# GpSimd makes the first norm's rows, half of the convolution and half of the softplus; two table loads fewer; scales read as pairs

## The reference, cut to what matters

```
x = x + tanh(g_xattn[0]) * attention(layernorm(x), ctx)      # softmax over 256 keys of each batch
x = x + tanh(g_ffn[0])   * ternary_ffn(layernorm(x))         # weights rounded to -s, 0, s; s = mean |w| of 64
x = x + tanh(g_xattn[1]) * ssm(ctx, z=layernorm(x))          # conv of 4 taps, silu, softplus, 16 states, scan
x = x + tanh(g_ffn[1])   * moe(layernorm(x))                 # 64 experts, top 8, capacity 128

# inside ssm
u     = silu(conv1d(in_proj_w @ ctx, conv_w, 4 taps, causal) + conv_b)
delta = softplus(dt_proj_w @ (x_proj_w @ u)[:8] + dt_proj_b)
# inside ternary_ffn, for each group of 64 weights
scale = clip(mean(abs(w)), 1e-8);  q = clip(round(w / scale), -1, 1);  w_hat = q * scale
```

## Time and profile before

| | us |
|---|---|
| median of 3 runs | 412.1 (411.82 to 413.02) |
| profiled execution, span | 411.6 |
| ACT busy | 263.1 |
| DVE busy | 305.4 |
| POOL busy | 260.1 |
| PE busy | 338.7 |

### The profile page before, as it was taken

How to read it: one execution, slowest core, us unless ns; L and a number is a source line. 1 busy time by engine, 2 the same in 40 slices (tenths; PEclk the granted TensorE clock), 3 DMA queues, 4 the chain that set the end, 5 groups by cost and what they waited for, 6 DMA issues and landing times.

```text
span 411.6 us, 7573 instructions
## 1 busy us (share of the span) xinstructions
PE 338.7 (82%) x2217; PEld 267.8 (65%) x2217; DVE 305.4 (74%) x694; ACT 263.1 (64%) x530; POOL 260.1 (63%) x213
## 2 busy tenths in 40 slices
PE   4945974698789799989885189999999999999980
PEld 2431663256566567666685178899998899899870
DVE  2999999979999999999888946554544535454365
ACT  0899999999888898888264344445445544554410
POOL 4200022679996897788423588778788787878730
PEclk9995895599999989989999579999999999999997
DMA  8930530577344877441198339899898989865557
GB/s 235 372 121 0 152 114 3 183 224 244 118 153 130 273 259 260 154 146 59 42 263 204 104 105 209 219 212 241 202 238 219 221 216 217 224 139 94 96 107 241
DMA packets 59132, 72.17 MB, mean 175 GB/s; under 512 B 6802, under 2 KB 43458, under 8 KB 59106
## 3 DMA queue, kind: packets, MB, share of 16 engines
q1 hardware_dynamic: 49104, 56.04, 44.2%
q0 software_dynamic: 8832, 15.74, 19.1%
q10 hardware_dynamic: 1170, 0.08, 0.3%
HBM read 61.75 MB, written 10.09 MB: 175 GB/s over the span
## 4 chain that ended last, share of the span: by engine, by line
PE 50%; ACT 15%; DVE 14%; DMA 12%; issue 5%; POOL 2%; SPq 1%; DVEq 0%; POOLq 0%; ACTq 0%
PE bank L1328 13%; PE bank L1366 10%; PE bank L1321 6%; PE bank L1162 5%; DMA ssm<-bc_rows 4%; PE bank L1308 3%; DVE bank L1565 3%; DMA B_last<-bc_rows 3%; ACT ssm L862 2%; ACT L862 2%; DVE ssm L1570 2%; ACT L900 2%; DMA du<-sums 2%; PE bank L1104 2%; PE bank L1314 1%
## 5 line engine op out<-in xcount | busy, mean ns | idle before, releaser
L602 POOL TENSOR_TENSOR ssm<-ssm,arena 128x1024 f32<-128x1024 f32 x31 | 73.2, 2360 | 18.8 <-DVE ssm L1570 9.3
L1570 DVE TENSOR_TENSOR_SCAN ssm<-ssm,bank 128x512 f32<-128x512 f32 x64 | 78.1, 1220 | 4.6 <-issue 2.3
L675 POOL DMA_INDIRECT ssm<-routed,idx x64 | 65.0, 1016 | 21.8 <-issue 14.6
L1793 DVE SCALAR_TENSOR_TENSOR ssm<-ssm,bank 128x96 f32<-128x96 f32 x64 | 20.1, 314 | 75.3 <-ACT ssm L974 75.0
L686 POOL DMA_INDIRECT sums<-ssm,idx x40 | 65.3, 1631 | 13.6 <-issue 10.4
L1328 PE MATMUL bank<-ssm,wguT 128*128 128x256 bf16 x576 | 72.4, 272 | 0.3 <-DVE ssm L1785 0.3
L1328 PEld LDWEIGHTS bank<-ssm,wguT 128*128 128x128 bf16 x576 | 56.0, 97 | 12.3 <-DVE ssm L1785 0.7
L974 ACT ACTIVATE ssm<-bank 128x96 f32<-128x96 f32 x64 | 16.1, 251 | 74.3 <-PE bank L1366 74.3
L1162 PE MATMUL bank<-xs,wguT 128*128 128x512 bf16 x192 | 49.4, 412 | 7.8 <-POOL xs L589 4.2
L1366 PE MATMUL bank<-arena,ssm 128*128 (+1 forms) x256 | 53.3, 331 | 1.8 <-ACT ssm L957 1.1
L862 ACT ACTIVATE ssm<-delta,A_sb 128x510 f32<-128x510 f32 x64 | 43.9, 714 | 6.1 <-DVE ssm L1570 5.9
(11 more groups left out here) (226 smaller groups left out, 667.9 us busy)
## 6 DMA issues: line engine op xcount, KB each, us to landing
ssm<-bc_rows SPq DMA_DIRECT2D x22, 512.0 KB, 3.8
arena<-bc_rows SPq DMA_DIRECT2D x16, 512.0 KB, 5.1
arena<-in_L_ffn_gate_proj SPq DMA_DIRECT2D x32, 192.0 KB
arena<-in_L_ffn_up_proj SPq DMA_DIRECT2D x32, 192.0 KB
arena<-in_L_ffn_down_proj SPq DMA_DIRECT2D x32, 192.0 KB
B_last<-bc_rows SPq DMA_DIRECT2D x10, 512.0 KB, 3.8
sums<-zero_f SPq DMA_DIRECT2D x1, 2304.0 KB, 14.0
arena<-in_L_ffn_w_gate_up SPq DMA_DIRECT2D x1, 2048.0 KB, 11.6
```

Source lines behind the costliest of these rows:

```text
L602: pool.tensor_tensor(prod[:, a:b, :], hs[:, a:b, :], C_all[:, 2 * (q % 8):2 * (q % 8) + 2, :], ALU.mult).then_inc(s.prod_ok, 1)
L675: pool.indirect_dma_start(out=xe[:, k, :], out_offset=None, in_=routed, in_offset=bass.IndirectOffsetOnAxis(ap=idx2[:, k, 0:1], axis=0)).t ...
L1570: dve.tensor_tensor_scan(hs[:, k % 4, :], dA[:, k % 3, :], x[:, :], 0.0, ALU.mult, ALU.add).then_inc(s.scan_ok, 1)
```

## The change

- Norm 1's rows are made by POOL (`normalise(c)`, four TENSOR_SCALAR of 256 columns for each chunk), between and behind the two `ln_rstd(1, ...)`. DVE's eight operations of L1415 are gone.
- `convolve_second` on POOL makes half 1 of the convolution: one TENSOR_SCALAR, then three pairs of TENSOR_SCALAR (a tap into `delta[:, 1]`, free then) and TENSOR_TENSOR (the sum), 1024 columns each, with waits between them. ACT's silu of half 1 waits for its semaphore.
- ACT's `spread` is gone. `q_scale` holds each scale twice, and `rest_and_mask` subtracts |w| from the scales read through an access pattern of (group step 2) x (32 times the same) x (2 adjacent bf16).
- `softplus_second` on POOL, between `ln_rstd(2, (0,))` and `ln_rstd(2, (1,))`: two TENSOR_SCALAR and two TENSOR_TENSOR of 1024 columns; behind `ln_rstd(2, (1,))` POOL also makes `delta[:, 1]` with a third TENSOR_TENSOR. DVE keeps half 0, moves `quantised(1)` ahead of `nmr` 1, and makes `delta[:, 0]` behind it.
- ACT loads a table by name at the very start (`exp_and_others`) and ahead of the softplus exponentials (`natural_log_exp_and_others`, which has Exp and Ln), so that the loads at L809 and at the first decay aren't needed. The decays of phase 0 wait for `delta[:, 0]` alone.

```diff
+            def normalise(c):
+                pool.wait_ge(s.ln_r, c + 1)
+                for j in range(4 * c, 4 * c + 4):
+                    pool.tensor_scalar(xn[j], x_res[:, j, :], mv[:, j, 0:1], rstd[:, j:j + 1], ALU.subtract, ALU.mult).then_inc(s.xn_sb, 1)
+            def convolve_second():
+                pool.wait_ge(s.ld_cols, 16 * 4)
+                pool.wait_ge(s.wT_sb, 3)
+                pool.wait_ge(s.xin_sb, 4)
+                ub, tap = (v[:, 1, :].rearrange("p (b l) -> p b l", l=L) for v in (u, delta))
+                for k in range(DC):
+                    src = xin[:, 1, :, k:k + L]
+                    if k == 0:
+                        pool.tensor_scalar(ub, src, conv_sb[:, 1, 0:1], cols[:, 1:2], ALU.mult, ALU.add).then_inc(s.conv_second, 1)
+                    else:
+                        if k > 1:
+                            pool.wait_ge(s.conv_second, 2 * k - 1)
+                        pool.tensor_scalar(tap, src, conv_sb[:, 1, k:k + 1], None, ALU.mult).then_inc(s.conv_second, 1)
+                        pool.wait_ge(s.conv_second, 2 * k)
+                        pool.tensor_tensor(ub, tap, ub, ALU.add).then_inc(s.conv_second, 1)
-            ln_rstd(1)
-            ln_rstd(2)
+            ln_rstd(1, (0,))
+            normalise(0)
+            ln_rstd(1, (1,))
+            normalise(1)
+            convolve_second()
+            def softplus_second():
+                pool.wait_ge(s.sp_exp, 2)
+                pool.tensor_single_scalar(Bbc[:, 1, :], delta[:, 1, :], 1.0, op=ALU.add).then_inc(s.sp_second, 1)
+                pool.wait_ge(s.sp_second, 1)
+                pool.tensor_single_scalar(Bbc[:, 1, :], Bbc[:, 1, :], -1.0, op=ALU.add).then_inc(s.sp_second, 1)
+                pool.wait_ge(s.sp_second, 2)
+                pool.tensor_tensor(Bbc[:, 1, :], Bbc[:, 1, :], delta[:, 1, :], ALU.subtract).then_inc(s.sp_second, 1)
+                pool.wait_ge(s.sp_second, 3)
+                pool.wait_ge(s.sp_relu, 4)
+                pool.tensor_tensor(Bbc[:, 1, :], du[:, 1, :], Bbc[:, 1, :], ALU.subtract).then_inc(s.sp_second, 1)
+            ln_rstd(2, (0,))
+            softplus_second()
+            ln_rstd(2, (1,))
+            pool.wait_ge(s.sp_second, 4)
+            pool.wait_ge(s.sp_ln, 2)
+            pool.tensor_tensor(delta[:, 1, :], Cbc[:, 1, :], Bbc[:, 1, :], ALU.add).then_inc(s.delta_second, 1)
...
+            act.preload_act_table_set("exp_and_others")
             act.wait_ge(s.c_pad, 1)
...
-            spread(0)
             for j in range(NT):
                 act.wait_ge(s.en_max, 2 * (j // 2) + 2)
...
             for h in halves:
-                act.wait_ge(s.conv, 4 * h + 4)
+                act.wait_ge((s.conv, s.conv_second)[h], (DC, 2 * DC - 1)[h])
                 act.activation(u[:, h, :], u[:, h, :], ACT.Silu).then_inc(s.u_sb, 1)
-            spread(1)
...
+            act.preload_act_table_set("natural_log_exp_and_others")
             for h in halves:
                 act.wait_ge(s.sp_abs, 2 * h + 2)
...
-            act.wait_ge(s.delta_sb, 2)
+            act.wait_ge(s.delta_sb, 1)
...
-                dve.wait_ge(s.q_mat, part2 + 1)
-                dve.tensor_tensor(q_v[:, t], q_v[:, t], q_abs[:, t], ALU.subtract).then_inc(s.q_step, 1)
+                dve.wait_ge(s.q_scales, 2 * part2 + 2)
+                dve.tensor_tensor(v_pairs[:, g], over_group(part2), q_pairs[:, g], ALU.subtract).then_inc(s.q_step, 1)
...
             statistics(2, x1, s.x1_sb, (0,))
-            softplus_rest(0, lambda: mean_over_deviation(2, 0))
+            softplus_first()
+            mean_over_deviation(2, 0)
             statistics(2, x1, s.x1_sb, (1,))
-            softplus_rest(1, lambda: mean_over_deviation(2, 1))
-            for h in halves:
-                dve.wait_ge(s.sp_c, 3 * h + 3)
-                dve.wait_ge(s.sp_ln, h + 1)
-                dve.tensor_tensor(delta[:, h, :], Cbc[:, h, :], Bbc[:, h, :], ALU.add).then_inc(s.delta_sb, 1)
             quantised(1)
+            mean_over_deviation(2, 1)
+            dve.wait_ge(s.sp_c, 3)
+            dve.wait_ge(s.sp_ln, 1)
+            dve.tensor_tensor(delta[:, 0, :], Cbc[:, 0, :], Bbc[:, 0, :], ALU.add).then_inc(s.delta_sb, 1)
```

More of the change, by code:

```diff
@@ L117, in __init__ @@
         self.sp_c = sem("sp_c")
+        self.sp_second = sem("sp_second")
+        self.delta_second = sem("delta_second")
         self.sp_ln = sem("sp_ln")
@@ L284, in build @@
         qg = q_abs.rearrange("p (g n) -> p g n", n=GROUP)
-        vg = q_v.rearrange("p (g n) -> p g n", n=GROUP)
+        in_pairs = "p (g n two) -> p g n two"
+        q_pairs, v_pairs = (v.rearrange(in_pairs, n=GROUP // 2, two=2) for v in (q_abs, q_v))
         q_groups = (slice(0, 16 * D // GROUP), slice(16 * D // GROUP, NG))
         q_sum = sb("q_sum", [P, NG])
-        q_scale = sb("q_scale", [P, NG], BF16)
+        q_scale = sb("q_scale", [P, NG, 2], BF16)
         stats = sb("stats", [P, NT, 6])
@@ L391, in over_group @@
             g = q_groups[part2]
-            return part(q_scale[:, g.start:g.start + 1], (1, g.stop - g.start), (0, GROUP))
+            return part(q_scale[:, g.start, 0:1], (2, g.stop - g.start), (0, GROUP // 2), (1, 2))
         s = Semaphores(sem)
@@ L859, in decay @@
                 th, h, n, t = of_step(k)
+                if k == DS:
+                    act.wait_ge(s.delta_second, 1)
                 if k >= 3:
@@ L1410, in _ @@
         def _(dve):
-            def normalise(n, c):
-                for j in range(4 * c, 4 * c + 4):
-                    dve.wait_ge(s.ln_r, 2 * n - 1 + j // 4)
-                    dve.tensor_scalar(xn[j], x_res[:, j, :], mv[:, j, 0:1], rstd[:, j:j + 1], ALU.subtract, ALU.mult).then_inc(s.xn_sb, 1)
             def statistics(n, update=None, updated=None, chunks=(0, 1)):
@@ L1444, in _, with convolve_first @@
             statistics(1)
-            normalise(1, 0)
-            normalise(1, 1)
             dve.wait_ge(s.ld_cols, 16 * 4)
             dve.wait_ge(s.wT_sb, 3)
-            def convolve(h):
-                dve.wait_ge(s.xin_sb, 2 * h + 2)
-                ub = u[:, h, :].rearrange("p (b l) -> p b l", l=L)
+            def convolve_first():
+                dve.wait_ge(s.xin_sb, 2)
+                ub = u[:, 0, :].rearrange("p (b l) -> p b l", l=L)
                 for k in range(DC):
-                    src = xin[:, h, :, k:k + L]
+                    src = xin[:, 0, :, k:k + L]
                     if k == 0:
-                        dve.tensor_scalar(ub, src, conv_sb[:, h, 0:1], cols[:, h:h + 1], ALU.mult, ALU.add).then_inc(s.conv, 1)
+                        dve.tensor_scalar(ub, src, conv_sb[:, 0, 0:1], cols[:, 0:1], ALU.mult, ALU.add).then_inc(s.conv, 1)
                     else:
-                        dve.wait_ge(s.conv, 4 * h + k)
-                        dve.scalar_tensor_tensor(out=ub, in0=src, scalar=conv_sb[:, h, k:k + 1], in1=ub, op0=ALU.mult, op1=ALU.add).then_inc(s.conv, 1)
+                        dve.wait_ge(s.conv, k)
+                        dve.scalar_tensor_tensor(out=ub, in0=src, scalar=conv_sb[:, 0, k:k + 1], in1=ub, op0=ALU.mult, op1=ALU.add).then_inc(s.conv, 1)
             def scales(part2):
@@ L1492, in quantised @@
                 dve.tensor_tensor(q_r[:, t], q_v[:, t], q_sign[:, t], ALU.mult).then_inc(s.q_step, 1)
-            convolve(0)
+            convolve_first()
             scales(0)
@@ L1508, in _, with softplus_first @@
             quantised(0)
-            def softplus_rest(h, meanwhile):
-                dve.wait_ge(s.sp_exp, h + 1)
-                dve.tensor_scalar(Bbc[:, h, :], delta[:, h, :], 1.0, None, ALU.add).then_inc(s.sp_c, 1)
-                dve.wait_ge(s.sp_c, 3 * h + 1)
-                dve.scalar_tensor_tensor(out=Bbc[:, h, :], in0=Bbc[:, h, :], scalar=-1.0, in1=delta[:, h, :], op0=ALU.add, op1=ALU.subtract).then_inc(s.sp_c, 1)
-                dve.wait_ge(s.sp_c, 3 * h + 2)
-                dve.wait_ge(s.sp_relu, 2 * h + 2)
-                dve.tensor_tensor(Bbc[:, h, :], du[:, h, :], Bbc[:, h, :], ALU.subtract).then_inc(s.sp_c, 1)
-                meanwhile()
+            def softplus_first():
+                dve.wait_ge(s.sp_exp, 1)
+                dve.tensor_scalar(Bbc[:, 0, :], delta[:, 0, :], 1.0, None, ALU.add).then_inc(s.sp_c, 1)
+                dve.wait_ge(s.sp_c, 1)
+                dve.scalar_tensor_tensor(out=Bbc[:, 0, :], in0=Bbc[:, 0, :], scalar=-1.0, in1=delta[:, 0, :], op0=ALU.add, op1=ALU.subtract).then_inc(s.sp_c, 1)
+                dve.wait_ge(s.sp_c, 2)
+                dve.wait_ge(s.sp_relu, 2)
+                dve.tensor_tensor(Bbc[:, 0, :], du[:, 0, :], Bbc[:, 0, :], ALU.subtract).then_inc(s.sp_c, 1)
             dve.wait_ge(s.tg_sb, 1)
```

14 lines of the change are left out of this document (4 added, 10 removed).

## The result

| | before | after |
|---|---|---|
| median, us | 412.42 (411.82 to 413.02) | 428.68 (428.31 to 429.18) |
| profiled execution, span, us | 411.6 | 426.9 |
| POOL busy, us | 260.1 | 303.1 |
| DVE busy, us | 305.4 | 304.2 |

The changed kernel is slower: ratio 1.0365, interval 1.0324 to 1.0406 (the quotient of the two medians, 1.0394, lies in the interval). The forecast was 412.7 with a range up to 416.5; the time lies 12 us above the range. The direction was among the rivals, the size was not: the dearest of them gave 421.

The account below looks back on a forecast made before the run. It took the preparation's chain through ACT, PE and DVE to `nmr` 1, then the scan on DVE, as the bound. Terms: -2.4 + (1.83 + 2.4) - 1.28 = +0.55, span 412.15, median 412.7 us; range 409.6 to 416.5.

Parts of the forecast that it names:

- The chain it followed: Preparation: ACT up to x_proj, then ACT, PE and DVE to `nmr` 1; its gain or loss reaches the end unchanged.
- rival (3): Quantiser on DVE: the paired read of the scales runs at single rate, +2.4 us on top, 415.1; chance 0.08.
- rival (5): Table loads on ACT: they stay because the compiler inserts its own, +1.28 us, 413.9; chance 0.04.
- The loads: ACT: dropping the load at the first decay gains 1.28 us; the one ahead of the logarithm is worth nothing.
- The gain at x_proj: First part: PE starts x_proj at 33.1 instead of 35.52 and ends it at 39.1, gain 2.4 us.
- POOL's one-input time: POOL's TENSOR_SCALAR: 0.4 us for 256 columns, 1.05 for 1024, with the two-input times as upper ends.
- Norm rows: Norm 1 on POOL: about 1.6 us, alternating with DVE's convolution, the second four ending at 21.8, no cost.
- Convolution: Half 1 on POOL: 11.6 us, from 21.8 to 33.4, its silu done at 34.4, just in time for PE.
- From the end of x_proj to that of `nmr` 1: Quantiser, softplus and norm 2: from 39.1 to 66.05, with `nmr` 1 a loss of 1.8 us against 64.22.
- The exclusive use of SBUF: POOL and DVE: with two SBUF inputs or a two-port mode, one waits for the whole of the other's operation.
- Rival (2): POOL's convolution comes late: DVE's quantiser goes first for 2.24 us, the last sum ends at 36.0; +2.95, 415.1; chance 0.21.
- Rival (4): One-input work on POOL costs what two-input does: convolution to 39 (+6.3), softplus +2.6, total 421; chance 0.04.

Follow-up runs that it names:

- experiment 10: Kernel before, with only the two table loads made by name: 411.56 us, ratio 0.9951.
- kernel 6: Changed kernel with every wide one-input POOL operation written as (multiply, add): 419.59 us, ratio 1.0145.
- kernel 8: Changed kernel with norm rows and softplus back on DVE; only the convolution stays on POOL, its taps as (multiply, add): 412.39 us, ratio 0.9969.
- kernel 11: kernel 5 with POOL making the first two taps and their sum as (multiply, add), after DVE's half 0: 408.82 us, ratio 0.9878.
- kernel 5: Changed kernel with all three POOL parts back on DVE, leaving the named loads and the paired scales: 409.77 us, ratio 0.9911.
- kernel 7: Changed kernel with POOL's delta of half 1 waiting until DVE has made `nmr` 1: 427.39 us, ratio 1.0323.
- kernel 3: Changed kernel with half 1 of the convolution back on DVE: 424.69 us, ratio 1.0309.

## Why the prediction failed

**The chain it followed was right.** From x_proj to `nmr` 1 to the first scan the work ran as laid out, and each delay of the preparation arrived at the end (15.85 at the first scan, 15.3 in the span). The pairs keep full rate (2.23 against a forecast of 2.24), so rival (3), and the rule that it quotes, are out for this read; no load stands at the logarithm or the first decay, so rival (5) is out. The loads are worth 1.31 at the end of the scan against 1.28, though not by way of the first scan (experiment 10). The gain at x_proj from taking `spread` away was sized at 2.4 and is 3.1 to 3.5 at its start without the POOL parts.

**The term that failed is POOL's one-input time**, 1.05 us for 1024 columns and 0.4 for 256, and with it the bounds. It was taken from a fill and a cast, which do no arithmetic, and the upper end was the two-input time, 2.36, in the belief that one input can't cost more than two. It does: 2.78 to 2.85, and 1.25 for 256 columns against an upper end of 0.77. `nmr` 1 ended 16.1 later than forecast (82.12 against 66.05): 13.0 of it are this price, 4.4 are holds at SBUF, 0.8 a slower x_proj product, and 2.1 went the other way. By the prediction's own steps:

- Norm rows: forecast free, with the second four ending at 21.8. Measured 5.0 for each four, the last at 25.6: POOL starts the convolution 3.8 late, and the energies on PE start at 26.79 instead of 22.17, behind transposes that waited for POOL row by row, and take 5.81 at a granted clock of 0.62 instead of 3.72 at 1.00. So the exponentials, for which `spread` had been taken away, start at 29.5, no earlier than before (29.2). Putting the rows back on DVE gave 8.1 in the spans (6.1 by the ratios), and the prediction had put them at no cost.
- Convolution: forecast 11.6. Alone it costs 1.19 + 3 x 2.85 + 3 x 2.35 + 0.5 = 17.3, which is 5.7 more, and 2.2 more were lost beside DVE (4.93 instead of 2.85, 2.53 instead of 2.34). So 3.8 + 5.7 + 2.2 = 11.7: it ends at 45.1 and not at 33.4. The rest of the x_proj product, at a granted clock of 0.50, took 0.8 more than laid out.
- From the end of x_proj to that of `nmr` 1: forecast 27.0 (39.1 to 66.05), measured 30.55 (51.57 to 82.12). Two one-input operations at 2.78 instead of 1.05 are 3.5 more and the held `nmr` 1 is 2.15 more. The way up to POOL's first softplus operation was 2.1 shorter than laid out (51.57 to 65.61, against 39.1 to 55.2): the first x1 came 8.7 after x_proj and not 9.2, the second pair didn't wait 0.82 for PE, and the power took 1.43 instead of 1.99.

**The exclusive use of SBUF was the right mechanism and was applied to too few operations.** Rival (2), that DVE's quantiser goes first and the convolution ends late, is what happened, in the cheap forms too, where DVE was 0.01 us ahead. It was priced as one hold of 2.24; in the cheap forms there were two in a row, 2.10 and 1.91. The `nmr` products were never put beside POOL's last sum: the prediction let `nmr` 1 and `delta[:, 1]` start on the same event, the end of the power, and costed the small one at its own 0.15 us. It is 2.30, on the path. Rival (4) named the right quantity but stopped at the two-input price, and for that gave 421 and a chance of 0.04. Its end of the convolution, 39, is what the true prices give from the forecast's start (21.8 + 17.3 = 39.1), since the first tap is cheap and the others dear; the 6 us up to 45.1 are the late start and the hold beside DVE, which it didn't have. Its "+6.3" is 5.6 by its own ends (39 against 33.4).

**Why POOL's help was no gain even at the right price.** In the cheap form (kernel 6) POOL's help still costs 10.0 us against leaving the work on DVE. Where two engines can't use SBUF together, moving an operation takes time off one list and can put a longer time, 2.34 for 1.22, on both. For the convolution that is measured: kernel 8 has DVE at 7.38 instead of 3.92. And kernel 11, whose POOL work lies beside operations that aren't held, has no such cost. For the norm rows and the softplus in the cheap form no run tells the hold from POOL's own length, but for the 2.15 of `nmr` 1.

The Trainium skill (GPSIMD Engine Reference, Engine selection) has one-input work "roughly line-rate"; the prediction leaned on it as fitting. The rows agree for (multiply, add) and the copy (1.04 to 1.19) and disagree for single operations and (subtract, multiply) (2.77 to 3.78).

**Left open.** The intervals don't separate kernel 11 from kernel 5, nor kernel 7 or kernel 3 from the changed kernel. Norm rows alone and softplus alone in the cheap form on POOL were not run.
